# One batch's sums moved ahead, fewer unread matmuls, earlier table loads and a later last ranking in a mixture-of-experts and attention kernel

## The reference

```python
x = x + 0.5 * ffn(layernorm(x))    # mixture of experts, top 2 of 8, hidden 512, exact gelu
x = x + attention(layernorm(x))    # 16 heads of 8, rotary embedding, softmax over 256 keys
x = x + 0.5 * ffn(layernorm(x))    # the same weights again
```

## Time and profile before

| what | value |
|---|---|
| time, median of 3 runs | 492.79 us |
| all three runs | 492.79, 488.77, 493.09 us |
| the profiled execution, its own time | 494.3 us |
| its span in the trace | 492.5 us |
| granted clock of PE, mean of that execution | 0.962 |
| PE busy | 405.1 us, 82% of the span |
| DVE busy | 355.2 us, 72% |
| ACT busy | 256.0 us, 52% |
| POOL busy | 213.9 us, 43% |

### The profile page before, as it was taken

The page is one execution under the profiler, slowest core; times in us unless marked ns, Lnnn a source line. Parts: engine busy times, 40 slices in busy tenths (PEclk is TensorE's granted clock), DMA queues, the critical chain, the costliest instruction groups (busy, mean ns, idle before and its releaser), DMA issues. The chain is left out here.

```text
span 492.5 us, 10357 instructions
## 1 busy us (share of the span) xinstructions
PE 405.1 (82%) x3224; PEld 331.3 (67%) x3224; DVE 355.2 (72%) x1148; ACT 256.0 (52%) x515; POOL 213.9 (43%) x268
## 2 busy tenths in 40 slices
PE   1542599999999986989988989899998999999910
PEld 1442388898798864666656666676587888888800
DVE  4798335646776858999999999886465755568856
ACT  2520256765556444666665746575565456555500
POOL 5488764583544311212113243424046658335531
PEclk9999999999999998899999999999799999999965
DMA  9612812123111015980000000001112121132331
GB/s 283 250 38 56 247 38 55 55 55 92 44 44 32 24 55 201 310 265 23 1 23 13 12 13 13 23 12 34 45 32 60 46 66 49 49 98 68 89 107 43
DMA packets 32691, 37.71 MB, mean 77 GB/s; under 512 B 4992, under 2 KB 27520, under 8 KB 32240
## 3 DMA queue, kind: packets, MB, share of 16 engines
q1 hardware_dynamic: 27632, 27.32, 18.7%
q0 software_dynamic: 4544, 9.35, 5.8%
q10 hardware_dynamic: 464, 0.38, 0.3%
HBM read 26.64 MB, written 20.36 MB: 95 GB/s over the span
## 5 line engine op out<-in xcount | busy, mean ns | idle before, releaser
L1187 ACT ACTIVATE stage<-ps 128x512 f32<-128x512 f32 x78 | 46.7, 598 | 81.1 <-PE ps L722 80.8
L1768 DVE TENSOR_REDUCE mx<-ps 128x4 f32<-128x1024 f32 x64 | 77.3, 1214 | 8.9 <-PE ps L835 8.8
L1654 DVE TENSOR_TENSOR ring_hi<-ps,ring_hi 128x512 fp32r<-128x512 f32 x78 | 53.9, 691 | 36.7 <-ACT ring_hi L1194 36.2
L1241 ACT ACTIVATE stage<-ps 128x1024 f32<-128x1024 f32 x64 | 65.5, 1023 | 26.7 <-PE ps L846 25.9
L745 PE MATMUL ps<-w_hl,ring_hi 128*128 x234 | 65.5, 348 | 0.9 <-DVE stage L1662 0.9
L499 POOL DMA_INDIRECT expert_y<-stage x39 | 38.9, 998 | 53.4 <-DVE stage L1662 52.7
L746 PE MATMUL ps<-w_hl,ring_hi 128*128 x312 | 61.1, 237 | 0.0
L480 POOL DMA_INDIRECT sorted_x<-rows,place_at x32 | 35.6, 1112 | 54.8 <-DVE place_at L1475 48.3
L1648 DVE TENSOR_TENSOR bx<-ps,bx 128x128 fp32r<-128x128 f32 x78 | 22.5, 288 | 50.1 <-ACT bx L1169 49.6
L499 POOL DMA_INDIRECT expert_y<-stage,arena x39 | 38.9, 996 | 42.9 <-DVE stage L1662 38.3
L746 PEld LDWEIGHTS ps<-w_hl,ring_hi 128*128 128x128 f32 x312 | 54.6, 193 | 0.0
(11 more groups left out here) (197 smaller groups left out, 1056.5 us busy)
## 6 DMA issues: line engine op xcount, KB each, us to landing
sorted_x<-fill SPq DMA_DIRECT2D x8, 1096.5 KB, 16.9
stage<-w SPq DMA_DIRECT2D x16, 256.0 KB, 6.7
y_got<-expert_y SPq DMA_DIRECT2D x24, 128.0 KB, 2.3
stage<-sorted_x SPq DMA_DIRECT2D x39, 64.5 KB, 1.8
arena<-sorted_x SPq DMA_DIRECT2D x39, 64.5 KB, 1.8
x_tok<-x SPq DMA_DIRECT2D x4, 256.0 KB, 4.9
sorted_x<-rows,place_at POOLq DMA_INDIRECT x64, 2.4
stage<-sel SPq DMA_DIRECT2D x1, 1024.0 KB
```

Of the source, the lines that this page charges most:

```text
L1187: act.activation(g_full[:, s, :], ps[:, H_BANK, :], ACT.Gelu).then_inc(g_done, 1)
L1241: act.activation(prob[:, 2 * v:2 * v + 2, :], ps[:, at:at + 2, :], ACT.Exp, scale=SCALE)\
L1654: vec.tensor_tensor(bg_lo[:, s, :, :].rearrange("p c n -> p (c n)"), ps[:, G_BANK, :], bg_hi[:, s, :, :].rearrange("p c n -> p (c n)").bit ...
L1768: vec.tensor_reduce(mx[:, t, :].rearrange("p (r g j) -> p r j g", r=2, g=2)[:, pair, 2 * jp:2 * jp + 2, :], ps[:, at:at + 2, :].rearrange( ...
```

## The change

Five edits, none of which changes what is computed:

1. DVE, `batch(0)`: sums and statistics of `combine(2)` stand between `maxima(1, 0)` and `maxima(1, 1)`, no more behind the latter.
2. PE, `batch(0)`: `keep_busy` before step 0 has 2 matmuls in place of 8, before step 1 it has 3 in place of 4, before `a_transpose_x(2)` it has 3 in place of 8.
3. ACT: an Exp of one column on a scratch tile `act_pad` at the end of slot 38 of the first expert phase, so that the Exp table is loaded there and not ahead of `exps(0, 0)`; and a Gelu of one column after `exps(7, 7)`.
4. PE, slot 7 of the second expert phase: `totals(3)` and the last `rank` move from `amid_second` to `beside_second`, that is from ahead of `turn_g` and `down` to behind them.
5. DVE, same slot: `rank_blocks(3)` stands ahead of the last `placing`, no more behind it.

```diff
@@ PE step
                 if v == 0:
                     pe.wait_ge(exp_done, STEPS * b + v + 1)
-                    keep_busy(EXP_BANK, 8 if b == 0 else 3)
+                    keep_busy(EXP_BANK, 2 if b == 0 else 3)
                 if scores_next:
                     scores_free(b + 1, v)
                 if b == 0 and v == 1:
-                    keep_busy(2, 4)
+                    keep_busy(2, 3)
@@ PE batch, ahead of a_transpose_x(b + 2)
                     else:
                         pe.wait_ge(exp_done, STEPS * b + 4 + EXP_BUF)
-                        keep_busy(EXP_BANK, 8)
+                        keep_busy(EXP_BANK, 3)
@@ PE beside_second
                 if s == 4:
                     rank(u - 1)
+                if s == 7:
+                    totals(3)
+                    rank(u)
@@ PE amid_second
                 if s == 6:
                     router(u)
-                if s == 7:
-                    totals(3)
-                    rank(u)
@@ ACT blocks
                         beside_second(s)
+                    if phase == 0 and s == SLOTS - 1:
+                        act.activation(act_pad[:, :], neg_half[:, 0:1], ACT.Exp)
@@ ACT batch
                 exps(b, 7)
+                if not place_next:
+                    act.activation(act_pad[:, :], neg_half[:, 0:1], ACT.Gelu)
@@ DVE batch
                 if place_next:
                     maxima(b + 1, 0)
+                if b == 0:
+                    combine(2, apply_part=False)
                 if place_next:
                     maxima(b + 1, 1)
-                if b == 0:
-                    combine(2, apply_part=False)
@@ DVE beside_second
                 if s == 7:
+                    rank_blocks(3)
                     placing(u)
-                    rank_blocks(3)
```

More of the change, by code:

```diff
@@ L174, in build @@
         pads = sb("pads", [P, 4])
+        act_pad = sb("act_pad", [P, 1])
         sched_pad = sb("sched_pad", [P, TABLES * PHASES])
```

## The result

The changed kernel takes 488.08 us (median of 15 runs, 485.9 to 493.4); the kernel before takes 492.3 us beside it (15 runs, 488.46 to 496.42). The ratio is 0.991, with a 95% interval of 0.9891 to 0.9929. In a second comparison it was 488.92 against 492.96, ratio 0.9942 (0.9909 to 0.9975). So the medians differ by 4.2 and 4.0 us, and the two ratios put the gain at 3 to 4.5 us. The forecast was 489.1 us, in a range of 486.2 to 492.6.

The account below looks back on a forecast made before the run. PE, busy for 82% of the span, was taken as the bound, losing only waits. Attention -4.3, row chain -1.05 and clock +1.7 gave -3.65 from the profiled 494.3; less 1.5 to the median, 489.1 us, range 486.2 to 492.6.

Parts of the forecast that it names:

- The begin of attention, -4.3: Batch 2's transpose starts 4.3 us earlier: 1.3 from fewer unread matmuls, 3.0 from DVE's sums no longer behind the maxima.
- The table load, 0: Loading the Exp table in ACT's idle time before the last `g_high` costs 0 and gains nothing further in the sum.
- PE's order in slot 7, -2.7: Second expert phase: PE no longer idles for the last picks, so `up` of slot 8 comes 2.7 us earlier.
- The row chain, -1.05: Last placing, scatters, landing, load: rows for slot 12 come 1.05 us earlier, so only 1.05 of 2.7 us stay.
- The clock behind that wait, +1.7: After PE's 2.2 us wait for rows at slot 12, one stretch at the lower clock costs 1.7 us, bounds 0 and 3.4.
- the clock holds at slot 12: Rival: the clock stays up after the wait for rows at slot 12; -5.35, 487.4 us, chance 0.30.
- The other low stretches, costed at 0: The low-clock stretch near the begin of attention changes by 0, bounds -3.4 (vanishes) and +1.7 (one more).
- The step to the median, -1.5: The profiled execution, 494.3 us, was taken as 1.5 us above the median of 492.79, so 1.5 comes off.
- Fewer unread matmuls bring the clock down sooner: Rival at the begin of attention: 12 fewer matmuls let the clock fall from step 1 on; +1.35, 494.1 us, chance 0.08.
- The prediction's sign: In the changed kernel's profile: one stretch at clock 0.50 behind attention's transpose, not before step 3.
- Half of it given back: Rival: DVE paces batch 0 or batch 2's loads land late, halving the attention gain; -1.5, 491.3 us, chance 0.20.
- the loads late: Rival: batch 2's data isn't there before unit 1's maxima, so 1.3 of 4.3 remains; -0.65, 492.1 us, chance 0.04.

Follow-up runs that it names:

- e6: The kernel before with only DVE's sums and statistics of `combine(2)` moved ahead of `maxima(1, 1)`; 492.08 us, ratio 0.9991.
- e7: The kernel before with only the unread matmuls cut to 2, 3 and 3 from 8, 4 and 8; 492.37 us, ratio 1.0007.
- e8: The changed kernel without the early one-column Exp, so the table loads ahead of the first exponential again; 487.56 us, ratio 0.9916 to the kernel before.
- e5: The changed kernel once more, nothing else changed; 488.92 us, ratio 0.9942 to the kernel before.
- e3: The changed kernel with slot 7's `placing` ahead of `rank_blocks(3)` again, on a slower chip; 506.84 us, ratio 0.9878 to the kernel before.
- e12: e3 repeated on another slower chip; 505.78 us, ratio 0.9887 to the kernel before.
- e9: The changed kernel plus six unread matmuls in slot 12 of the second phase, on a slower chip; 511.04 us, ratio 0.9982 to the kernel before.
- e1: The kernel before with the attention and table-load edits, slot 7 as before, slower chip; 510.04 us, ratio 0.9854 from three runs.
- e4: The changed kernel with 8 unread matmuls, not 3, ahead of batch 2's transpose, slower chip; 509.63 us, ratio 0.9919 to the kernel before.
- e2: The kernel before with only the two slot 7 edits (PE's order, `rank_blocks` ahead of placing), slower chip; 511.88 us, ratio 0.9976.
- e11: e2 repeated on another slower chip; 511.5 us, ratio 1.0013 to the kernel before.
- e10: e9 with also 8 unread matmuls, not 3, ahead of batch 2's transpose; 509.14 us, ratio 0.9956 to the kernel before.

## Why the prediction was right, and where not

*The begin of attention, -4.3: right, and by its steps.* 17.11 became 12.88, 12.86 and 12.87 in three executions: 4.25 us less. The sums were foretold for 180.2 (180.18) and the transpose for 187.4 (187.38). That the two parts add to 4.3 only when both are made (e6, e7) the prediction didn't say; it took the 8 matmuls of the third group as cut already.

*The table load, 0: right* (e8: transpose at 12.87 without the early load). The prediction named a drain of 1.38 us that the Trainium skill gives (ScalarE: Activation LUTs, What ACT_TABLE_LOAD costs). The changed kernel's rows don't show it either: the load ends at 170.10 and the activation starts at 170.12, in e8 at 180.47 and 180.49.

*PE's order in slot 7, -2.7: right* on the first kind of chip, 6.13 to 3.40. *The row chain, -1.05: mis-sized.* It gave 1.91 in the first profile. The first scatter of rows came 1.20 earlier relative to up(46) (8.33 to 7.13), near the 1.05; the last one landed in 2.28 us where the earlier trace rows have 2.99, 0.71 more. So PE waited 1.70, not 2.2. In e5 and e8, with 2.04 and 2.10 of wait, the 2.2 was nearly met.

*The clock behind that wait, +1.7: right in two executions of three.* It is the term that the prediction set apart as its first rival, "the clock holds at slot 12", at 487.4 us. In the first profiled execution the clock held. That this execution took 487.33 us is luck: the rival's 487.4 is a median, and from the profiled 494.3 its -5.35 gives 488.95; 0.86 more came by the row chain and 0.71 by attention behind the transpose. In e5 and e8 the clock fell, as forecast, and cost 1.62 and 1.63. Both medians of the changed kernel, 488.08 and 488.92, lie between the rival's number and the forecast's 489.1, as a mixture of the two would, but the other low stretches move the time as much, so the medians don't show it. The weak step is that one answer was taken for a thing that goes either way from execution to execution. With both terms together the forecast had edits 4 and 5 cost 0.65 us; against before they gained 2.00, 0.04 and lost 0.03.

*The other low stretches, costed at 0: they are the largest scatter.* The changed kernel's first profile has one of 10.3 us at the begin of attention, longer than that of the earlier trace rows, a second that the kernel before doesn't have (1.00 from 200 to 346), and none at 346.2:

```profile
185.60:195.90 10.30, 9.39 (x57) 6.87 (x59) 9.06 (x14) 3.51 (x5) 1.70 (x3) 0.50 1.05 340
...
305.00:308.60 3.60, 3.56 (x22) 3.44 (x22) 2.92 (x6) 0.59 (x2) 1.11 (x3) 0.53 0.06 18
...
346.20:353.20 7.00, 6.03 (x78) 3.46 (x78) 2.47 (x20) 5.51 (x11) 1.07 (x3) 1.00 0.21 52
```

The kernel before has 0.51 at that time, though with other instructions, since it is 5 us behind there:

```profile
346.20:353.20 7.00, 6.44 (x41) 4.03 (x44) 3.75 (x25) 2.17 (x3) 1.07 (x3) 0.51 0.31 77
```

and e5, the changed kernel again, even longer:

```profile
346.40:356.70 10.30, 9.95 (x70) 5.06 (x74) 2.54 (x16) 5.64 (x11) 1.05 (x3) 0.51 0.15 34
```

By the table e5 loses 1.93 + 1.92 = 3.85 us to the first profile around there (up(39), the begin of the second expert phase, is at 352.24 in e5), with the same instructions. This is as much as the whole change gives. From transpose to up(39) the first profile is 0.71 shorter than before (163.56 and 162.85), e5 1.24 longer. The Trainium skill (TensorE: Matmul & The Clock Gate, What's actually happening) says of the start of a kernel that the number of matmuls at the lower clock differs between runs of the same kernel. These profiles show the like in the midst of one, with the 3.85 us between two executions.

*The step to the median, -1.5: too small in itself and made up for.* The kernel before has its median at 492.3 over 15 runs, so its profiled execution was 2.0 above. 494.3 - 3.65 - 2.0 is 488.65, and both medians are within 0.6 us of that; that they are so near is in part luck: the profiled executions of the changed kernel differ by 5.9 us in their spans (485.5 and 491.4) through stretches costed at 0.

*Fewer unread matmuls bring the clock down sooner:* in these profiles it fell sooner, at 185.6 in place of 192.8, so that three of them took 1.43 us. The prediction's sign, a stretch that begins behind the transpose (187.38), was missed by this. But it began behind step 3 (183.68), and the transpose came when DVE was ready. The rival's condition, a fall ahead of step 1, was not met. *Half of it given back* and *the loads late* fell with the table's first two lines.

*What the prediction overlooked is edit 5.* It saw that `rank_blocks` ahead of the placing lets the placing end only 0.9 us earlier, and went on. That the old order would let the rows' first scatter start 1.5 to 1.7 us sooner could be worked out from the same rows; e3 and e12 show it.

## What to carry to other kernels

Cost an edit against the next-latest engine, and then ask whether another edit of the same change moves that one: e6 and e7 give 1.9 and 1.3 us alone and 4.25 together. When engine A is given its work earlier, look at what engine B has ahead of the one result that others wait for; here 1.9 us of ranking ahead of a 0.7 us placing put the first scatter of rows off by 1.70 us. When a profile names a releaser that it can't tell ("remote"), look for another instruction with the same label whose waits the code narrows down; here a gelu that waits for PE alone has it too, so the y scatters aren't the cause. A change of 4 us can't be read from one profile each where one stretch at the lower clock moves the same kernel by 3.9: use intervals between named instructions for the mechanism, and medians for the time.

## What the runs showed of the hardware

- The same kernel takes 492 to 493 us on one kind of chip and 512 to 513 on two other chips. There ACT's gelu of block 46 starts 4.7 us behind the start of the last matmul that it waits for (e9: 382.94 to 387.61) in place of 0.4, with an idle bracket of 4.46 to 5.63 us in all eight traces, and up(46) to up(52) takes 24 to 28.5 us against 19 to 21. Why is open. The begin of attention is 12.85 to 12.89 us there with edits 1 to 3 (e1, e3, e4, e9, e12) and 17.16 and 17.17 without (e2, e11): the same gain on all three chips.
- A wait of 1.70 us in full PE work left the granted clock at 1.00; waits of 2.04 and 2.10 in the same place were followed by 3.3 to 3.6 us at 0.50 to 0.53, at a cost of 1.6 us. One execution each is not a bound.
- Unread matmuls are no safe cover: eight of them took 2.11 us in e4 and 3.42 in e10, where the clock fell while they ran, and six took 2.76 in e9 where there was no wait to fill.
- POOL's scatter starts 0.30 us behind its predecessor when all is there. Behind a placing that has just ended it takes longer: in the changed kernel the placing ends at 378.24 and the scatter starts at 379.05, 0.81 later. In the kernel before, a placing that ends at 372.88 is followed by the scatter of the earlier trace rows at 373.70, 0.82 later.
